# Cross attention: the first pair's contexts loaded as rows only and turned by TensorE

## The reference, cut to what matters

```python
def xattn(hidden_states, memory_tokens, memory_mask):      # (32,64,512), (32,256,512), (32,256)
    scores = einsum('bsd,bmd->bsm', hidden_states, memory_tokens) / sqrt(512)
    scores = where(memory_mask[:, None, :], scores, -1e30)
    attn = softmax(scores)
    out = einsum('bsm,bmd->bsd', attn, memory_tokens)
    return where(any(memory_mask)[:, None, None], out, 0)
x = x + xattn(layernorm(x), ctx_2048, mask)
x = x + attn(layernorm(x), ...)     # latent attention with 16 heads
x = x + ffn(layernorm(x), ...)
```

## Time and profile before

| | |
|---|---|
| median of 3 runs | 1027.86 us (1027.06 to 1028.83) |
| time of the profiled execution | 1027.9 us |
| its span, first to last instruction | 1026.1 us |
| mean granted TensorE clock | 0.996 |
| busy: PE, PEld, DVE, ACT, POOL | 98%, 80%, 51%, 31%, 31% |
| HBM | 81.99 MB read, 20.97 MB written |

### The profile page before, as it was taken

One profiled execution on the slowest core, in us unless ns is written; L12 is line 12 of the kernel. 1 busy time (PEld: TensorE's weight loads), 2 busy tenths in 40 slices (PEclk: granted clock), 3 DMA queues, 4 the chain that ended last, 5 costly groups with the idle time before them and its releaser, 6 DMA issues.

```text
span 1026.1 us, 19038 instructions
## 1 busy us (share of the span) xinstructions
PE 1001.1 (98%) x7490; PEld 816.8 (80%) x7490; DVE 522.9 (51%) x973; ACT 322.5 (31%) x586; POOL 315.9 (31%) x369
## 2 busy tenths in 40 slices
PE   5899999999999999999999989999999999999997
PEld 3677786788888888888888868888888888888886
DVE  3666657556555575556556673545413541353115
ACT  3455645323222222222222332432222232213220
POOL 2344366242222311142214212442323232323232
PEclk9999999999999999999999998999999999999999
DMA  9999986131004310341033423412022102200201
GB/s 359 412 420 399 394 346 157 24 73 33 22 22 99 73 27 22 82 93 27 19 92 74 159 68 83 154 51 63 1 93 62 52 1 93 83 31 1 82 1 42
DMA packets 66491, 112.58 MB, mean 110 GB/s; under 512 B 15018, under 2 KB 35781, under 8 KB 61925
## 3 DMA queue, kind: packets, MB, share of 16 engines
q1 hardware_dynamic: 64676, 107.44, 32.0%
q10 hardware_dynamic: 1728, 3.93, 1.0%
HBM read 81.99 MB, written 20.97 MB: 100 GB/s over the span
## 4 chain that ended last, share of the span: by engine, by line
PE 92%; DVE 3%; issue 2%; POOL 1%; ACT 1%; DMA 1%; SPq 0%; DVEq 0%; ACTq 0%; POOLq 0%
PE b_z L47 8%; PE b_z L49 8%; PE b_z L48 8%; PE b_turn L47 5%; PE b_turn L48 5%; PE b_turn L49 5%; PE b_score L47 4%; PE b_score L49 4%; PE b_score L48 4%; PE b_prob L47 4%; PE b_prob L48 4%; PE b_prob L49 4%; PE b_read L48 4%; PE b_read L47 4%; PE b_read L49 4%; PE b_score L629 3%
## 5 line engine op out<-in xcount | busy, mean ns | idle before, releaser
L1608 POOL TENSOR_TENSOR f_hT_lo<-f_h,f_hT_hi 128x512 fp32r<-128x512 f32 x64 | 83.2, 1300 | 209.5 <-ACT f_hT_hi L1670 199.7
L1755 DVE TENSOR_TENSOR f_h<-f_h 128x512 f32<-128x512 f32 x64 | 45.6, 712 | 132.6 <-ACT f_h L1663 132.6
L47 PE MATMUL b_z<-m_zT_lo,m_wq_hi 128*128 128x512 f32 x192 | 78.0, 406 | 0.5 <-ACT m_qT L919 0.4
L49 PE MATMUL b_z<-m_zT_hi,m_wq_hi 128*128 128x512 f32 x192 | 74.9, 390 | 0.0
L48 PE MATMUL b_z<-m_zT_hi,m_wq_lo 128*128 128x512 f32 x192 | 74.9, 390 | 0.0
L875 POOL TENSOR_TENSOR m_sc<-m_sc,m_causal 128x512 f32<-128x512 f32 x16 | 22.0, 1373 | 163.1 <-DVE m_sc L1025 163.1
L919 ACT ACTIVATE m_qT<-b_z,m_q_bias 128x512 f32<-128x512 f32 x64 | 43.7, 685 | 59.3 <-PE b_z L49 59.3
L860 POOL TENSOR_TENSOR m_qpe<-m_qpe,m_swapped 128x512 f32<-128x512 f32 x32 | 41.3, 1289 | 57.6 <-DMA m_swapped<-m_by_sin 57.6
L1670 ACT CAST f_hT_hi<-f_h 128x512 fp32r<-128x512 f32 x64 | 39.9, 623 | 57.1 <-DVE f_h L1755 57.1
L881 POOL TENSOR_TENSOR m_sc<-m_sc,m_rs 128x768 f32<-128x768 f32 x16 | 23.7, 1484 | 106.6 <-DVE m_rs L1056 106.6
L1663 ACT ACTIVATE f_h<-b_turn 128x512 f32<-128x512 f32 x32 | 19.2, 599 | 110.4 <-PE b_turn L49 110.4
(11 more groups left out here) (278 smaller groups left out, 2897.2 us busy)
## 6 DMA issues: line engine op xcount, KB each, us to landing
x_ctx_in<-ctx_rows_dram SPq DMA_DIRECT2D x16, 1024.0 KB, 14.7
x_ctxT<-ctx_turned_dram SPq DMA_DIRECT2D x15, 1024.0 KB, 14.8
m_swapped<-m_by_sin SPq DMA_DIRECT2D x128, 64.0 KB, 2.0
m_raw<-attn_raw_dram SPq DMA_DIRECT2D x6, 768.0 KB, 10.7
x_x_all<-x_dram SPq DMA_DIRECT2D x16, 256.0 KB, 15.4
m_z_in<-z_scratch SPq DMA_DIRECT2D x16, 256.0 KB, 4.0
m_x<-x_scratch SPq DMA_DIRECT2D x16, 256.0 KB, 4.8
x_scratch<-m_x SPq DMA_DIRECT2D x16, 256.0 KB, 4.0
```

What stands on the lines that cost most here:

```text
L47: nc.tensor.matmul(out, lh, rl, start=first, stop=False)
L49: return nc.tensor.matmul(out, lh, rh, start=False, stop=last)
L1608: q.tensor_tensor(hT_lo[k % 6][:], h[:, k % 2], hT_hi[k % 6][:].bitcast(F32), ALU.subtract).then_inc(s["h_lo"], 1)
L1755: v.tensor_tensor(h[:, k % 2], h[:, k % 2], h[:, k % 2], ALU.mult).then_inc(s["squared"], 1)
```

## The change

The two half loads of pair 0's `ctxT` become two half loads of its `ctx_in`, at the same places in SyncE's order, and the later full load of `ctx_in` of pair 0 is gone. TensorE turns the 16 blocks of 128x128 (`flip`, between `turn0(0)` and the slots) into the banks z0, z1, free and turn1, one bank for each feature block k. ScalarE copies the banks of k = 0 and 2 into `ctxT`, VectorE those of k = 1 and 3. The score of pair 0 waits for these copies in place of the loads.

```diff
-        "... w_loaded ctxT_first0 ctxT_first1 "
+        "... w_loaded ctx_first "
...
-        "scored maxed ...
+        "flipped flip_act flip_dve scored maxed ...
+    b_flip = [banks.z0, banks.z1, banks.free, banks.turn1]
...
-        def first_ctxT(h):
-            sp.dma_start(ctxT[:, 0, 2 * h:2 * h + 2], A["ctx_turned"][0, :, 2 * h:2 * h + 2]).then_inc(s[f"ctxT_first{h}"], 16)
+        def first_ctx(h, done):
+            sp.dma_start(ctx_in[:, 0, 2 * h:2 * h + 2], A["ctx_rows"][0, :, 2 * h:2 * h + 2]).then_inc(s[done], 16)

         load_x(0)
-        first_ctxT(0)
+        first_ctx(0, "ctx_first")
         load_x(1)
-        first_ctxT(1)
+        first_ctx(1, "ctx_loaded0")
         sp.dma_start(mask_u8[:], A["mask_BxS2_bk0"]).then_inc(s["masks_loaded"], 16)
...
         load_x(2)
         load_ctxT(1)
-        load_ctx(0)
         load_x(3)
...
         norm(0, 0, xn0, x_all[:, 0])
         turned0(0)
+        for k in (0, 2):
+            act.wait_ge(s["flipped"], k + 1)
+            a.copy(ctxT[:, 0, k], b_flip[k][:]).then_inc(s["flip_act"], 1)
         slots(slot)
...
         v.tensor_scalar(mask_rows[0:BATCH], mask_u8[:], BIG, -BIG, ALU.mult, ALU.add).then_inc(s["masks_built"], 1)
+        for k in (1, 3):
+            dve.wait_ge(s["flipped"], k + 1)
+            v.tensor_copy(ctxT[:, 0, k], b_flip[k][:]).then_inc(s["flip_dve"], 1)
         slots(slot)
...
+        def flip():
+            half = CTX // P
+            for b, landed in enumerate(("ctx_first", "ctx_loaded0")):
+                pe.wait_ge(s[landed], 16)
+                for k in range(KH):
+                    for c in range(half * b, half * b + half):
+                        last = t.transpose(b_flip[k][:, P * c:P * c + P], ctx_in[:, 0, c, P * k:P * k + P], ident[:])
+                    if b:
+                        last.then_inc(s["flipped"], 1)
...
-                if p == 0 and k % 2 == 0:
-                    pe.wait_ge(s[f"ctxT_first{k // 2}"], 16)
+                if p == 0:
+                    pe.wait_ge(s[("flip_act", "flip_dve")[k % 2]], k // 2 + 1)
...
         pe.wait_ge(s["consts"], 3)
         turn0(0)
+        flip()
         slots(slot)
```

More of the change, by code:

```diff
@@ L244, in stage_x @@
     s = {n: ctx.enter_context(nc.semaphore("x_" + n)) for n in (
-        "x_loaded0 x_loaded1 x_loaded2 x_loaded3 x_loaded4 x_loaded5 masks_loaded small_loaded w_loaded ctxT_first0 ctxT_first1 "
+        "x_loaded0 x_loaded1 x_loaded2 x_loaded3 x_loaded4 x_loaded5 masks_loaded small_loaded w_loaded ctx_first "
         "ctxT_loaded0 ctxT_loaded1 ctxT_loaded2 ctxT_loaded3 ctx_loaded0 ctx_loaded1 ctx_loaded2 ctx_loaded3 x1_first x1_rest "
@@ L248, in stage_x @@
         "stats0 var0 eps0 rstd0 shift0 norm0 turned0 xT0 stats1 var1 eps1 rstd1 shift1 norm1 turned1 xT1_hi xT1_lo "
-        "scored maxed exped inverted validated p_turned pT "
+        "flipped flip_act flip_dve scored maxed exped inverted validated p_turned pT "
         "read x1_done z_made z_biased squared q_var q_rstd q_scaled z_parts z_kv z_rope").split()}
```

## The result

The changed kernel takes 1030.2 us (median of 20 runs, 1025.91 to 1032.81), against 1027.05 us of the kernel before beside it (20 runs, 1024.45 to 1029.06). The ratio is 1.0022, 95% [1.0012, 1.0032]: slower by 1.2 to 3.3 us. That is inside the range of the prediction and has the sign of its sum. It also lies just beyond the 0.2% for which the prediction gave no change a chance of 0.72; slower had 0.20.

The account below looks back on a forecast made before the run. Idle TensorE ahead of 40 us, set by a chain of engines rather than transfers, then TensorE itself bounds the kernel. 1027.9 + 1.37 = 1029.3 profiled, so 1029.2 us forecast; range 1026.6 to 1030.7.

Parts of the forecast that it names:

- Loads: Start: halves land at 5.5 and 8.4 us, `picks` at 9.14 again; nothing taken for the 1 MB less.
- TensorE: Start: 16 transposes from 7.54 to 10.95 us without waiting for transfers; 1.37 us of them on the path.
- Copies: Start: ScalarE and VectorE copies, 0.59 and 0.68 us each, finish before the score wants them; they cost nothing.
- Queues behind the waits: Start: pair 1's norm on ScalarE and later VectorE and POOL work stay hidden, with over 1 us of room.
- Bytes: Start: 1 MB less brings later transfers 2.5 us sooner, worth at most 0.02 us on the path; nothing taken.
- the third rival: Start is bound by transfers after all: up to 2.5 us come back, 1025.4 us; chance 0.08.
- with TensorE's level coming as late behind the score's start as before: Start: pair 0's score still takes 3.68 us at the lower clock, so everything from it on shifts by 1.37 us.
- The lower bound of that term: Start: upper clock level as soon as transposes end, score 1.95 us in place of 3.68, sum -0.36 us.
- the first rival: Start: the transposes lift TensorE's clock, giving -0.36 us, or 1027.5 us; chance 0.27.
- TensorE full from about 41 us, and every stage after it as long as before: Rest of the kernel after the start: nothing absorbs or adds to the shift of 1.37 us.

Follow-up runs that it names:

- before_warm: Kernel before with 24 identity transposes ahead of TensorE's first turn: 1028.79 us, 1.0007 of the kernel before.
- before_2: Kernel before, unchanged, measured once more: 1027.66 us, ratio 0.9996.
- after_lean: Changed kernel less 32 TensorE waits that other waits imply, so its program has the old length: 1026.94 us, 0.9988 of the kernel before.
- after_2: Changed kernel, unchanged, measured once more: 1029.44 us, 1.0014 of the kernel before.
- after_3: Changed kernel, unchanged, measured again in a later series: 1030.3 us, 1.0019 of the kernel before.
- idle_flip_2: Kernel before with old loads plus 16 transposes into idle banks nobody reads, second series of the same file: 1030.78 us, 1.0021 of the kernel before.
- before_pad32: Kernel before with 32 idle instructions at the head of TensorE's program: 1030.1 us, 1.0022 of the kernel before.
- idle_flip: Kernel before with old loads plus 16 transposes into idle banks nobody reads, first series: 1027.41 us, 0.9995 of the kernel before.
- after_pad48: Changed kernel with 48 more idle TensorE instructions, 80 over the kernel before: 1027.93 us, 1.0004 of the kernel before.
- after_warm: Changed kernel with 24 identity transposes ahead of TensorE's first turn: 1026.79 us, 0.9995 of the kernel before.

## Why the prediction was right or wrong

**Right.** *Loads*: foreseen at 5.5 and 8.4, landed at 6.1 and 8.5; `picks` at 9.1 as foreseen. No transpose waited for a half. *TensorE*: 16 transposes at 0.213 us, foreseen to leave TensorE free at 10.95; the next matmul started at 11.02. *Copies*: VectorE's took 0.69 us (0.68 taken), ScalarE's 0.59, the last ended at 11.95 and none was waited for, though the score ran at the upper level. *Queues behind the waits*: the norm of pair 1 ran at 11.31 and nobody waited. *Bytes*: worth nothing as the start stands. That the third rival's mechanism is real, behind a cover of about 2 us, `before_warm` shows.

**Wrong, at the start.** The step "with TensorE's level coming as late behind the score's start as before", worth +1.37 us. The level came with TensorE's work, transposes too: the clock record rises at 11.32, 10.88 and 12.74 us in the three profiles of the change, 14.05 and 14.08 in two of before. The score took 1.95, 1.95 and 2.51 us. The work at 46 us is shifted by -0.25, -0.39 and +0.49 us, not +1.37. The lower bound of that term, -0.36, was what happened in two of the three, and with it the first rival's mechanism; in the third the rise came in the middle of the score. Where its chance went wrong: I gave most weight to the earlier trace rows, where short matmuls went on at the lower level after an idle gap, and too little to the rise between the first two scores. The first is a fall and its sequel, the second a start.

**Wrong, after the start.** The step "TensorE full from about 41 us, and every stage after it as long as before". Here the loss arises, and neither the sum nor a rival had it. The prediction counted what 32 more instructions do in time, not what they do to the place of everything behind them. The stall near 595 us was 1.22, 0.91 and 0.63 us where the program has its old length (before, `before_2`, `after_lean`), mean 0.92. It was 1.39, 1.94, 3.03, 1.66, 2.97 and 2.48 us where it is 32 instructions longer, mean 2.25. That is 1.3 us more. More time at half clock is the other part. If each low run (26 of 44 of the three series of after) holds one further stretch of 1.7 us, it is 1.0 us; by the mean clocks, which lie lower by 0.0015 in `after_2` and `after_3` than in the runs of before beside them, it is 1.5 us. Together that estimates 2.3 to 2.8 us, from six profiles against three; the ratios of the three series (1.0022, 1.0014, 1.0019) are 2.3, 1.4 and 2.0 us. The size is met roughly, and how it splits between stall and clock is not shown for the timed runs. The two profiles with as much time at half clock as before, `after_3` and `idle_flip_2`, show the stall's part by itself: they lose 1.9 and 1.3 us between 590 and 603 us and keep it to the end.

So the number lay in the range and the sign was right, by luck: 1.37 us that did not come, and some 2 us that were not foreseen. The chances did less well: no change within 0.2% had 0.72, and the ratio fell just outside of it.

That the length of the program is the cause, through the place of the cut, is shown from both sides: the loss without the change (`before_pad32`), the change without the loss (`after_lean`), and the stop at the same instruction by number in every profile. That the fetch packet is what TensorE waits for is read from the 2.2 to 2.5 us between the two, and was not changed by itself. The stall varies from 1.39 to 3.03 us at one place because the packet starts 1.1 us before TensorE runs out of work (after) or as much as 0.7 us behind (`after_3`); why it starts so differently is open. Open too is when the clock falls: the first series of `idle_flip` has the cut of the change and did not lose time (0.9995, 2 of 11 low runs), its second did (1.0021, 9 of 12), and `after_pad48` has a stall of 1.55 us and no low run. A stretch at 1.2 GHz right behind the stall stands in the profiles of `after_2` and `idle_flip`; no execution of the change at a mean clock of 0.994, as 16 of the 44 were, was profiled.

## What to carry to other kernels

When an engine is full for a millisecond, an edit at one end moves the program's cuts at the other: where a few instructions more or less give a change of 0.2%, look at the stalls without a releaser and at their place, and try the same edit with the program's length kept or padded before blaming it. Take more than one profile: those of after, `after_2` and `after_3`, all of the same kernel, end 1.7 us ahead of before, 1.1 and 2.2 behind. Waits that others imply are a cheap source of instructions to give back. Matmuls in the time in which TensorE waits for its first data brought the upper clock early, and 1.7 us at 46 us; look then at the transfers, which have to keep up with the earlier start, and at what is left of it at the end, here nothing that the timed runs could tell.

## What was not expected of the hardware

- Crossing from one fetched piece of the program to the next costs TensorE 0.4 to 3.0 us near 595 us of this kernel (`after_warm` and `after_3`): 2.2 to 2.5 us from the start of the packet, less the work that TensorE still has at that time. The Trainium skill ("Runtime: NRT & Kernel Launch", Instruction fetch mechanics) has blocks of 256 instructions, whose crossing is "mostly hidden". The size agrees with the 61 packets of 1.00 MB. Hidden it was only in part here: 1.1 to 1.7 us behind nine long matmuls, and from nothing to 1.9 us (`after_warm`) in a burst of short ones.
- TensorE's level of 2.4 GHz was there after 24 transposes (rise at 4.95 us, first of them at 1.53), and a gap of 1.94 us in TensorE's work was followed, 1.7 us later, by 3.4 us at 1.2 GHz (`after_2`), one of 3.03 us at the same place was not (`after_3`).
- A wait that is met at once is not free at the head of a program: 80 idle instructions put off the first turn by 3.1 us, while 32 put off the work at 46 us by 0.6.
- The clock column reads 1.00 from the start of the span, though the same 16 matmuls take 3.68 us there and 1.95 us later: ahead of its first record the column says nothing.
